# A recurrent cell with a hyperbolic transformer block: attention groups leave the projection steps, and the tails of two pairs of batches share their chains of small operations

## What is computed

```python
def step(h, xt):                       # h starts as cond
    m = concat([xt, h]) @ weight + bias        # weight 256 x 256
    c = tanh(m[:, 128:]); g = sigmoid(m[:, :128] + 1.0)
    h_new = g * h + (1.0 - g) * c
x = x + scan(step)                     # 256 steps, 8 batches side by side
# block, with t_emb = cond; six vectors of 128 per batch from t_emb @ w_ada + b_ada
xm = expmap0(layer_norm(logmap0(x)) * (1 + sc_msa) + sh_msa)
q, k, v = to_heads(plin(xm, w, b)) for w, b in (q, k, v)   # 16 heads of 8
attn = softmax(qt @ kt.T / sqrt(8))    # over all 256 tokens, no mask
attn_t = g_msa * logmap0(plin(from_heads(expmap0(attn @ vt)), w_o, b_o))
x1 = mobius_add(x, expmap0(attn_t))
xm = expmap0(layer_norm(logmap0(x1)) * (1 + sc_mlp) + sh_mlp)
ff = plin(plin(xm, w_f1, b_f1), w_f2, b_f2)
out = x + mobius_add(x1, expmap0(g_mlp * logmap0(ff)))
```

## Time and profile before

| | us |
|---|---|
| median of 3 runs | 466.47 (466.36 to 471.59) |
| the profiled execution | 465.22 |
| its span (first to last instruction) | 463.4 |
| mean granted clock of TensorE | 0.933 of full |
| busy: TensorE, VectorE, ScalarE, GpSimd | 356.3, 313.8, 220.0, 79.3 |

### The profile page before, as it was taken

The page is one execution under the profiler, slowest core; times in us unless marked ns, Lnnn a source line. Parts: engine busy times, 40 slices in busy tenths (PEclk is TensorE's granted clock), DMA queues, the critical chain, the costliest instruction groups (busy, mean ns, idle before and its releaser), DMA issues.

```text
span 463.4 us, 14020 instructions
## 1 busy us (share of the span) xinstructions
PE 356.3 (77%) x5250; PEld 247.6 (53%) x5250; DVE 313.8 (68%) x1975; ACT 220.0 (47%) x986; POOL 79.3 (17%) x151
## 2 busy tenths in 40 slices
PE   1999899898857896857998999978489888835500
PEld 1745676566745675646666566645345455524500
DVE  6454444576777776788776477663932498899985
ACT  2123422225436424436446345756588898744231
POOL 6000000012000012000012000014200215546652
PEclk9999999999999999999999999999769999796555
DMA  7200940001000000000000000000000000000001
GB/s 181 60 1 4 192 84 3 2 8 43 1 1 3 3 2 1 2 2 1 2 3 3 1 3 2 4 1 3 1 2 3 1 3 3 1 9 17 1 23 45
DMA packets 9114, 8.41 MB, mean 18 GB/s; under 512 B 1276, under 2 KB 7694, under 8 KB 9047
## 3 DMA queue, kind: packets, MB, share of 16 engines
q1 hardware_dynamic: 8950, 7.26, 6.8%
q0 software_dynamic: 96, 0.26, 0.2%
HBM read 6.45 MB, written 1.08 MB: 16 GB/s over the span
## 4 chain that ended last, share of the span: by engine, by line
PE 59%; DVE 22%; ACT 10%; issue 5%; POOL 3%; DMA 1%; SPq 0%; DVEq 0%; POOLq 0%; ACTq 0%
PE zb L789 22%; PE tb L906 5%; PE tb L736 4%; PE zb L767 4%; PE firsts L962 4%; DVE prod_hi L1477 3%; PE firsts L946 3%; ACT state L1202 3%; PE firsts L1077 3%; PE tb L883 2%; ACT prd L1358 2%; PE zb L1057 2%; PE zb L773 2%; ACT state L1205 2%; PE firsts L789 2%
## 5 line engine op out<-in xcount | busy, mean ns | idle before, releaser
L789 PEld LDWEIGHTS zb<-prod_hi,whh 128*128 128x128 f16 x1920 | 72.5, 106 | 89.9 <-DVE prod_hi L1477 83.7
L1202 ACT ACTIVATE state<-zb 128x8 f32<-128x8 f32 x240 | 42.6, 177 | 155.9 <-PE zb L789 155.4
L789 PE MATMUL zb<-prod_hi,whh 128*128 128x8 f16 x1920 | 90.6, 171 | 33.3 <-DVE prod_hi L1477 32.7
L1477 DVE SCALAR_TENSOR_TENSOR prod_hi<-state 128x16 f16<-128x16 f32 x255 | 44.5, 175 | 87.3 <-ACT state L1205 84.7
L789 PE MATMUL zb<-prod_lo,whh 128*128 128x8 f16 x960 | 63.8, 172 | 0.0
L1483 DVE TENSOR_TENSOR prod_lo<-prod,prod_hi 128x16 f16<-128x16 f32 x255 | 44.6, 175 | 8.7
L789 PEld LDWEIGHTS zb<-prod_lo,whh 128*128 128x128 f16 x960 | 44.5, 107 | 1.1
L1358 ACT ACTIVATE prd<-zb 128x640 f32<-128x640 f32 x64 | 41.8, 711 | 6.2 <-PE zb L1057 5.5
L1479 DVE SCALAR_TENSOR_TENSOR prod<-state 128x16 f32<-128x16 f32 x256 | 43.3, 169 | 0.3 <-ACT state L1205 0.3
L1205 ACT ACTIVATE state<-zb 128x16 f32<-128x16 f32 x240 | 42.9, 179 | 0.0
L1485 DVE SCALAR_TENSOR_TENSOR state<-prod 128x8 f32<-128x8 f32 x256 | 41.0, 160 | 0.0
(11 more groups left out here) (333 smaller groups left out, 687.3 us busy)
## 6 DMA issues: line engine op xcount, KB each, us to landing
mod<-ada_rows SPq DMA_DIRECT2D x4, 768.0 KB, 11.4
resid<-in_x_dram SPq DMA_DIRECT2D x6, 128.0 KB, 3.7
ffz<-shift_rows SPq DMA_DIRECT2D x4, 131.0 KB, 3.5
out_dram<-state SPq DMA_DIRECT2D x8, 64.0 KB, 2.1
out_dram<-early SPq DMA_DIRECT2D x8, 64.0 KB, 2.1
yy<-in_L_cond_w_ada_dram SPq DMA_DIRECT2D x1, 384.0 KB
early<-in_L_cond_weight_dram SPq DMA_DIRECT2D x2, 128.0 KB
resid<-in_x_dram POOLq DMA_DIRECT2D x2, 128.0 KB, 3.4
```

The costliest lines, as they stand in the source:

```text
L789: i = pe.matmul(z_bank(t, k)[:, NB * (t % CH):NB * (t % CH) + NB], whh[:, half, p, k, :], src[:, NB * p:NB * p + NB], start=False, stop=Fa ...
L1202: act.activation(r[:, 24:32], z_bank(t, 1)[:, k:k + NB], ACT.Tanh, scale=-1.0 / ZS)
L1477: dve.scalar_tensor_tensor(prod_hi[:, :], r[:, 16:32], 1.0, r[:, 0:16], ALU.add, ALU.mult).then_inc(hi_ready, 1)
```

## The change

No function changes but one constant in att_groups; the tables are new.

- BUSY, the ticks that no group may use, grows from 193-196, 218, 219 by 220 to 227, and the first group's tick is 197 instead of 190. 24 groups instead of 29 come before tick 256, and 8 are late instead of 3. The groups now have the ticks 197, 199, ... 215, 228, 230, ... 254.
- PAIRS is ((0, 1), (2,), (3,)): pairs 0 and 1 share one tail, whose small operations work on 8 columns instead of 4.
- All the ticks behind the scan are new.

```diff
 TAIL0 = dict(
-    ot=(530, 553), o=(542, 564), oT=(575,), oevac=(586,), wo=(596,), m=(612,), wosq=(622,),
-    asq=(656,), adot=(622,), norm=668, tanh=699, mob=701, ascale=(729,), root=736, x2=(735,),
-    v=(747,), vtrans=(759,), vevac=(771,), vsq=(781,), artanh=758, lin=(822,), rho=823,
-    t6=(807,), g=(830,), gy=(850,), gdot=(841,), usum=850, clip2=869, fq=861, e=(870,), f1=888,
-    clip3=900, y=(899,), f2=(923,), f2sq=(967,), ffsq=(979,), fdot=(948,), norm3=991,
-    fftanh=1024, mob2=1028, ffscale=(1063,), out=(1078,), add=(1121,), artanh_=(767, 769, 771,
...
+    ot=(544, 576, 679, 702), o=(556, 586, 691, 713), oT=(596, 730), oevac=(607, 743), wo=(614,
+    751), m=(633, 769), wosq=(659, 796), asq=(688, 830), adot=(642, 779), norm=842, tanh=870,
+    mob=873, ascale=(896, 930), root=906, x2=(905, 934), v=(946, 965), vtrans=(963, 1069),
+    vevac=(989, 1079), vsq=(994, 1095), artanh=976, lin=(1051, 1113), rho=1051, t6=(1013, 1086),
+    g=(1022, 1096), gy=(1104, 1117), gdot=(1054, 1117), usum=1125, clip2=1137, fq=1136, e=(1152,
+    1166), f1=1179, clip3=1217, y=(1218, 1231), f2=(1248, 1302), f2sq=(1259, 1314), ffsq=(1277,
+    1326), fdot=(1294, 1337), norm3=1338, fftanh=1369, mob2=1372, ffscale=(1431, 1443),
+    out=(1449, 1491), add=(1466, 1505), artanh_=(979, 994, 996, 999, 1001, 1003, 1005, 1009,
...
 TAIL1 = dict(
-    ot=(676, 700), o=(688, 711), oT=(721,), oevac=(758,), wo=(781,), m=(797,), wosq=(806,),
...
+    ot=(842, 865), o=(855, 878), oT=(888,), oevac=(925,), wo=(938,), m=(957,), wosq=(966,),
...
 TAIL2 = dict(
-    ot=(868, 891), o=(882, 911), oT=(928,), oevac=(951,), wo=(960,), m=(983,), wosq=(997,),
...
-TAIL3 = dict(
-    ot=(1014, 1022), o=(1024, 1033), oT=(1048,), oevac=(1059,), wo=(1067,), m=(1089,),
...
+    ot=(996, 1005), o=(1007, 1016), oT=(1030,), oevac=(1041,), wo=(1055,), m=(1074,),
...
 DIAG = dict(
-    scores=(372, 378, 389, 398, 400, 412, 421, 430, 435, 445, 451, 461, 463, 476, 477, 487, 492,
...
-    945, 956, 962, 991), saved=(461, 514, 595, 668, 761, 851, 933, 1006), before=(81, 86, 93,
...
-    378), late=(36, 54, 67), late_exps=(48, 60, 73), late_values=(45, 60, 73, 80),
-    late_saved=(87,))
-TAILS = (TAIL0, TAIL1, TAIL2, TAIL3)
-PAIRS = ((0,), (1,), (2,), (3,))
+    scores=(396, 399, 409, 417, 420, 431, 437, 446, 449, 459, 465, 475, 477, 490, 491, 501, 506,
...
+    919, 941, 947, 959), saved=(475, 528, 597, 671, 754, 830, 915, 989), before=(146, 151, 158,
...
+    398, 404), late=(36, 54, 67, 80, 93, 106, 119, 132), late_exps=(47, 58, 74, 87, 100, 112,
+    125, 138), late_values=(46, 66, 73, 86, 99, 110, 125, 137, 145), late_saved=(61, 105, 151))
+TAILS = (TAIL0, TAIL1, TAIL2)
+PAIRS = ((0, 1), (2,), (3,))
...
-BUSY = frozenset((193, 194, 195, 196, 218, 219))
+BUSY = frozenset((193, 194, 195, 196, 218, 219, 220, 221, 222, 223, 224, 225, 226, 227))
...
 def att_groups():
...
-    out, t = [], 190
+    out, t = [], 197
```

More of the change, by code:

```diff
@@ L101 @@
-TAIL1 = dict(
-    ot=(676, 700), o=(688, 711), oT=(721,), oevac=(758,), wo=(781,), m=(797,), wosq=(806,),
-    asq=(829,), adot=(806,), norm=841, tanh=875, mob=880, ascale=(928,), root=959, x2=(958,),
-    v=(969,), vtrans=(985,), vevac=(1019,), vsq=(1025,), artanh=980, lin=(1064,), rho=1065,
-    t6=(1031,), g=(1039,), gy=(1081,), gdot=(1068,), usum=1077, clip2=1156, fq=1130, e=(1167,),
-    f1=1178, clip3=1188, y=(1188,), f2=(1209,), f2sq=(1221,), ffsq=(1232,), fdot=(1239,),
-    norm3=1247, fftanh=1275, mob2=1292, ffscale=(1325,), out=(1334,), add=(1376,), artanh_=(991,
-    1001, 1003, 1005, 1012, 1015, 1017, 1019, 1021, 1023, 1027, 1036, 1043, 1045, 1048, 1052,
-    1055, 1059, 1061, 1063, 2482), mob_=(885, 893, 895, 897, 910, 913), ss_=(919, 939, 947,
-    957), usum_=(1101, 1120, 1129), fq_=(1145, 1164, 1160), f1_=(1181, 1184, 1187), mob2_=(1295,
-    1299, 1303, 1307, 1310, 1322), ffm=(1221,), o_=(692, 715), out_=(2818, 2826, 2834))
@@ L112 @@
-TAIL2 = dict(
-    ot=(868, 891), o=(882, 911), oT=(928,), oevac=(951,), wo=(960,), m=(983,), wosq=(997,),
-    asq=(1008,), adot=(992,), norm=1020, tanh=1047, mob=1050, ascale=(1079,), root=1139,
-    x2=(1132,), v=(1146,), vtrans=(1158,), vevac=(1177,), vsq=(1182,), artanh=1157, lin=(1279,),
-    rho=1280, t6=(1184,), g=(1201,), gy=(1218,), gdot=(1281,), usum=1291, clip2=1301, fq=1302,
-    e=(1313,), f1=1325, clip3=1342, y=(1345,), f2=(1365,), f2sq=(1376,), ffsq=(1389,),
-    fdot=(1390,), norm3=1407, fftanh=1437, mob2=1439, ffscale=(1476,), out=(1488,), add=(1500,),
-    artanh_=(1163, 1166, 1176, 1180, 1183, 1186, 1197, 1200, 1205, 1208, 1219, 1258, 1262, 1264,
-    1266, 1268, 1271, 1273, 1276, 1278, 3258), mob_=(1054, 1058, 1060, 1062, 1067, 1076),
-    ss_=(1097, 1118, 1127, 1131), usum_=(1293, 1297, 1300), fq_=(1305, 1311, 1308), f1_=(1327,
-    1329, 1333), mob2_=(1443, 1446, 1448, 1450, 1463, 1470), ffm=(1383,), o_=(889, 915),
-    out_=(3594, 3602, 3610))
@@ new lines @@
+TAIL1 = dict(
+    ot=(842, 865), o=(855, 878), oT=(888,), oevac=(925,), wo=(938,), m=(957,), wosq=(966,),
+    asq=(977,), adot=(980,), norm=990, tanh=1020, mob=1023, ascale=(1045,), root=1067,
+    x2=(1064,), v=(1082,), vtrans=(1127,), vevac=(1137,), vsq=(1142,), artanh=1110, lin=(1267,),
+    rho=1266, t6=(1164,), g=(1178,), gy=(1195,), gdot=(1277,), usum=1286, clip2=1303, fq=1293,
+    e=(1326,), f1=1336, clip3=1368, y=(1350,), f2=(1385,), f2sq=(1396,), ffsq=(1414,),
+    fdot=(1430,), norm3=1438, fftanh=1468, mob2=1489, ffscale=(1526,), out=(1530,), add=(1547,),
+    artanh_=(1116, 1127, 1129, 1131, 1143, 1145, 1148, 1181, 1194, 1208, 1211, 1214, 1230, 1242,
+    1244, 1246, 1259, 1261, 1263, 1265, 2614), mob_=(1027, 1030, 1032, 1035, 1037, 1039),
+    ss_=(1042, 1046, 1050, 1063), usum_=(1288, 1290, 1292), fq_=(1313, 1325, 1318), f1_=(1345,
+    1347, 1349), mob2_=(1501, 1511, 1515, 1519, 1521, 1523), ffm=(1408,), o_=(859, 883),
+    out_=(2950, 2958, 2966))
@@ new lines @@
+TAIL2 = dict(
+    ot=(996, 1005), o=(1007, 1016), oT=(1030,), oevac=(1041,), wo=(1055,), m=(1074,),
+    wosq=(1084,), asq=(3070,), adot=(1093,), norm=1103, tanh=1130, mob=1133, ascale=(1154,),
+    root=1184, x2=(1183,), v=(1195,), vtrans=(1270,), vevac=(1289,), vsq=(1294,), artanh=1206,
+    lin=(1315,), rho=1293, t6=(1296,), g=(1337,), gy=(1354,), gdot=(1360,), usum=1369,
+    clip2=1384, fq=1378, e=(1396,), f1=1407, clip3=1419, y=(1418,), f2=(1439,), f2sq=(1454,),
+    ffsq=(3622,), fdot=(1472,), norm3=1482, fftanh=1511, mob2=1513, ffscale=(3710,),
+    out=(1541,), add=(3750,), artanh_=(1210, 1213, 1215, 1217, 1228, 1241, 1243, 1245, 1247,
+    1258, 1260, 1262, 1264, 1266, 1269, 1276, 1285, 1287, 1289, 1291, 3390), mob_=(1137, 1142,
+    1144, 1146, 1149, 1151), ss_=(1162, 1176, 1180, 1182), usum_=(1371, 1374, 1377), fq_=(1380,
+    1395, 1384), f1_=(1413, 1415, 1417), mob2_=(1516, 1520, 1522, 1525, 1527, 1529),
+    ffm=(1460,), o_=(1010, 1019), out_=(1553, 1564, 3742))
```

56 lines of the change are left out of this document (23 added, 33 removed), and 6 rows, old and new, of the table scores.

## The result

The changed kernel takes 469.36 us (median of 20 runs), the kernel before 466.23 in runs on the same chip; the ratio is 1.0081 [1.0061, 1.0100], that is 3.8 us. The ratio leaves out executions in a slower state, such as one of 514.54 us here, and is not the quotient of the two medians, which is 1.0067 (3.1 us). The kernel is slower, where 1.5 us less was forecast, and its time lies above the range. The profiled execution took 468.38 us with a span of 466.6, against 465.22 and 463.4: +3.2, near both. I split it at the same places as the prediction did. The columns are: when it happens in the trace of before and of after, and how the stretch up to it changed.

What follows compares the result with a forecast made beforehand. It took the scan's loop, then TensorE and ScalarE in the attention, then VectorE from about 400 us as bounds. Terms -5.2 + 2.5 - 3.9 + 5.2 - 1.3 + 1.2 = -1.5 us gave 464.9 us, range 461.0 to 468.5.

Steps and rivals of the forecast that it cites:

- Step 3: Diagonals, first scores to last save: 13 instead of 17 TensorE tail pieces and one tanh fewer on the way, -3.9 us.
- Step 2: Between scan and diagonals: five more late groups cost 6.8 us, partly covered by TensorE's 3.73 us hole, leaving +2.5 us.
- Step 1: Scan: groups leave seven of chunk 2's projection steps, 1.81 to 1.15 us each, and tick 190; -5.2 us together.
- The prediction's own sign: Forecast wrong if the scan keeps its length, last save isn't 5 us earlier, or the rest isn't some 5 us longer.
- Step 5: GpSimd's power grows 148 ns a column; the merged pair's 16-column norms take about 2.9 us and delay mob2, +1.2 us.
- Step 4: VectorE behind the last save: pair 0's large work comes after it, +5.2 us, less 1.3 taken up by free time.
- The other moves have one answer: Remaining moves put at no cost: new bank turns keep VectorE's order, pair 0's store goes later but far ahead of the last.
- A: Rival: TensorE's hole disappears, VectorE's gaps take 2.2 us, norms hidden, clock may stay at 2.4; -4.6 us, 461.9; chance 0.23.
- C: Rival: scan projection steps stay at 1.8 us because something other than the group fills them; +3.1 us, 469.6; chance 0.04.
- B: Rival: GpSimd's wide norms, two smaller powers and strict queues delay the end; +3.5 us, 470.0; chance 0.20 with its half.

Runs made afterwards that it cites:

- experiment 1: Kernel before with only the groups' new ticks, the new order of diagonals and four unmerged tails: 465.99 us, ratio 1.0006.
- experiment 4: Changed kernel, power in both norms of the merged tail on pair 0's 8 columns only, plain maximum for pair 1: 467.90 us, ratio 1.0050.
- experiment 5: Changed kernel, only the merged pairs' first norms narrowed to pair 0's 8 columns, third norms still 16 wide: 468.94 us, ratio 1.0077.
- experiment 9: Changed kernel, first and third merged norms each split into two halves of 8 columns, pair 2's output transfers issued by ScalarE: 466.60 us, ratio 1.0020.
- experiment 10: Kernel before with the new group ticks, diagonals and all four tails in the old order 24 ticks later: 464.41 us, ratio 0.9980.
- experiment 8: Changed kernel, merged first norms split into two halves of 8 columns, pair 2's output transfers issued by ScalarE: 466.33 us, ratio 1.0013.
- experiment 2: Kernel before with only the merge of pairs 0 and 1 and the changed kernel's tails, 17 ticks later: 471.72 us, ratio 1.0096.
- experiment 6: Kernel before, 21 small VectorE operations of tail 0's artanh chain left out: 464.08 us, ratio 0.9973.
- experiment 7: Kernel before, 21 small VectorE operations of tail 1's artanh chain left out: 464.78 us, ratio 1.0007.
- experiment 3: Changed kernel, pair 2's four output transfers issued by ScalarE instead of SyncE: 467.22 us, ratio 1.0026.

## Why the forecast was wrong, step by step

The sum was off by 4.7 us on the profiled executions (-1.5 against +3.2). The largest part of it is the end of the span, 2.1 us put at nothing; steps 3, 2 and 1 missed by 1.4, 1.1 and 0.4. Without the first of these the time would have been within the range. The prediction's own sign had said it too: it was to be wrong if the last save isn't 5 us earlier, and it was 3.8. By its steps:

- **Step 1, scan, -5.2: right.** Seven steps of 1.15 and the 191st at 1.07 were there; -4.8 with 0.4 lost on the ticks that I had called the same in kind.
- **Step 2, start of the diagonals, +2.5: undersized, 3.6 measured**, within its bounds. The five late groups were 6.8 us, as worked out. What failed is "chunk 3's token chain runs on VectorE and GpSimd as ever": the copy at the end of the hole came 3.0 later too, so the hole covered 3.2 and not 4.3. And 3.6 was a favourable execution: experiments 1, 4, 5, 9 and 10, with the same instructions up to there, began the diagonals at 337.4 to 337.6, which makes this term 4.3 to 4.6, outside the bounds. Together steps 1 and 2 leave -1.2 here and -0.25 to -0.4 there (experiment 10 by its ratio: -0.9, with an interval from -2.0 to 0). This is a nearly even trade: a group took 1.3 us in two projection steps and takes 1.36 behind the scan.
- **Step 3, diagonals, -3.9: oversized, 2.5 measured.** The pieces of work did go, but the first norms of the merged pairs, which I had priced only in the bound of step 5, held up ScalarE's exponentials for 1.96 us. Experiments 5 and 8, in which that power is narrower, have the save 1.6 and 2.4 us earlier. Their clock was higher too (0.62 and 0.95 in one, 0.57 and 1.00 in the other from 388 to 396, against 0.50), so that the two causes aren't told apart. Little of it reached the end: 0.2 by the ratio in experiment 5, 0.8 at VectorE's last operation in experiment 8.
- **Step 4, VectorE behind the last save: right with step 5 (+5.1 forecast, +4.85 measured).** It is right by its parts too: VectorE's busy time from the last save to its last operation grew from 52.8 to 58.1 us (+5.3, forecast +5.2); stops of 0.68 and 0.99 us went (forecast -1.3); one of 1.33 ahead of mob2 (forecast +1.2) and one of 0.39 for TensorE came. Experiment 2, with +6.65 for the same tails, shows that the sum depends on what TensorE does there. The saving in instructions (77, exactly) came with a deferral of pair 0's large work, and the deferral is what the end sees. That the chains removed "lie mostly in time that VectorE had free" fits with tail 1's fifteen operations behind the save, which were worth nothing; for those ahead of the save experiments 6 and 7 leave it open, since the clock changed with them.
- **Step 5, the wide power: right in size** (2.93 and 3.01 us against 2.9; 1.33 of waiting against 1.2). What it costs at the end is not sure: experiments 4 and 5 are 1.4 and 0.2 us below the changed kernel, with intervals that overlap its own. The two rows from which I took 148 ns a column are of two lines (L682 and L604), not of one as I wrote, but of the same operation, and the 16 columns bear them out. By the page's rule of the Trainium skill (GPSIMD Engine Reference, section 3.1) the term would have been nil; the trace doesn't agree for this power.
- **"The other moves have one answer ... pair 0's store goes later but far ahead of the last": the step that failed, +2.1 in the profile, 2.0 to 2.6 by experiment 3.** It is right about pair 0 and doesn't look at pair 2, whose add went behind pair 3's out. I followed the moved steps through the orders of VectorE and GpSimd and not through SyncE's.
- **The rivals.** A's condition came true in part (the hole went) and its result did not: the clock fell to 0.50 all the same. Windows of the changed kernel, where the earlier trace rows had 0.50 behind the hole:

```profile
304.00:308.00 4.00, 3.41 (x36) 1.45 (x36) 3.19 (x20) 1.79 (x3) 0.18 (x1) 0.50 0.02 4
312.00:316.00 4.00, 3.74 (x55) 2.10 (x55) 0.00 (x0) 2.67 (x14) 1.79 (x4) 0.50 0.01 4
...
332.00:336.00 4.00, 3.22 (x52) 2.18 (x44) 3.30 (x8) 3.12 (x10) 1.94 (x4) 0.50 0.00 0
```

  So the fall didn't hang on the hole: with 3.73 us of it the clock was 0.69 from 328 to 332, with 0.95 us it was 0.50. The Trainium skill (TensorE: Matmul & The Clock Gate, section on the HAM clock gate) says that activity releases the clock; here it fell and stayed there while TensorE never stood for more than 1.0 us at a time. In number C (+3.1, 469.6) was nearest, by luck: the projection steps did fall to 1.15. B (+3.5) was next, and it was right in mechanism for the waits on the two wide norms; behind the save the stops of VectorE show none for the smaller powers that it counted, and what brought the time near to it were the transfers, which it doesn't have.
- **What could be told.** I took 9.3 us for what a measurement of this kernel can tell from no change; the interval of the result is 0.9 us to either side.

VectorE takes 61.5 to 63.3 us from the last save to its last operation in the kernels with merged tails. Its work is not what grows: it is busy for 58.1 to 58.3 us in all of them. Its free time does, from 3.5 us in the changed kernel to 4.0 in experiments 4 and 9 and 5.0 in experiments 2, 5 and 8. In experiments 2, 4, 5 and 8 there is a wait of 1.1 us for products with Wo at the 1.2 GHz level and one of 0.8 instead of 0.4 for further products; in experiment 9 there is one of 0.8 for the latter and one of 1.37 for GpSimd. The wait before mob2 (1.33) has shrunk to 0.28 in experiment 4 and gone in experiment 9. What stays open is why the clock fell where it did, and so how much of an earlier save would be passed on if it didn't.

## What to carry to other kernels

Merging the small operations of two work items saves instructions, but it makes the earlier item wait for the later one. What counts is where the earlier item's large work lands: here it left a stretch in which VectorE had stops of 1 to 4 us for one in which it was busy for 58 of 61.5 us. A result that becomes ready late must be checked against every queue that it goes through to the end, the output queue first: two items that end together cost the last one the issue time of the other. And a move that takes work out of a loop and puts it behind the loop has both prices in the trace before it is made; at 1.3 against 1.36 us a group only the idle time that it fills is won.

## What the runs showed of the hardware

- **GpSimd's power grows by the column.** 4 columns 1.09 us, 8 columns 1.68, 16 columns 2.93 to 3.01, while an operation of VectorE takes 0.16 us on 4 columns and 0.17 on 8 (440.21 in the changed kernel).
- **A busy VectorE is not a bound VectorE.** Small operations start 0.08 us apart but are recorded with 0.16 us each, so that fifteen could go from a stretch that was 96% busy and nothing came earlier (experiment 7).

- **The cost of issuing.** An output transfer of 64 KB costs its queue 0.64 us to issue, so eight on one queue hold the last of them for 5.15 us; on a second queue four of them cost nothing that was seen.
- **The clock of TensorE as a cost.** The same eight products took 2.08 us at the 1.2 GHz level and 1.16 at 2.4, in two kernels that differ by 21 small operations of another engine; in experiment 5 VectorE waited 1.11 us for such products and in the changed kernel, at 2.4, it didn't. But not every fall costs. Up to the diagonals the instructions are the same in the changed kernel and in experiments 1, 3, 4, 5, 8, 9 and 10. The changed kernel and experiments 3 and 8 had 0.50 from 308 to 312 us, the other five 1.00, and the diagonals began at 336.6 to 336.9 in the one case and at 337.4 to 337.6 in the other. So the low level cost that stretch nothing; why it ended earlier there isn't shown.
